# A two-layer graph kernel: the output's normalisation on ScalarE, and a new order of the work around it

## What is computed

```python
# layer 0
mi, mj = x @ Wi.T, x @ Wj.T                  # 512 x 512 each
out = deg[:, None] * (mi + b) + a @ mj       # deg = row sums of a
h = layernorm(x + out)
# layer 1: 8 heads of 64
q, k, v = h @ Wq.T + bq, h @ Wk.T + bk, h @ Wv.T + bv
scores = (q @ k.T) / 8, masked where adj == 0
out = softmax(scores) @ v
y = layernorm(h + out @ Wo.T + bo)           # the output
```

## Time and profile before

| | |
|---|---|
| median of 3 runs (lowest, highest) | 2925.93 us (2925.61, 2926.91) |
| the profiled execution: its own time | 2926.99 us |
| its span, first to last instruction | 2925.2 us |
| granted TensorE clock, mean over the span | 0.996 |
| busy: PE / PEld / DVE / ACT / POOL | 97% / 84% / 77% / 64% / 64% |
| one step in the middle (1496.46 to 1541.22) | 44.76 us |
| store of 512 KB (`out<-hb`), issue to landing, median | 2.8 us |

### The profile page before, as it was taken

One profiled execution on the slowest core, in us unless ns is written; L12 is line 12 of the kernel. 1 busy time (PEld: TensorE's weight loads), 2 busy tenths in 40 slices (PEclk: granted clock), 3 DMA queues, 4 the chain that ended last, 5 costly groups with the idle time before them and its releaser, 6 DMA issues.

```text
span 2925.2 us, 59805 instructions
## 1 busy us (share of the span) xinstructions
PE 2845.6 (97%) x18584; PEld 2457.2 (84%) x18584; DVE 2258.0 (77%) x5774; ACT 1871.2 (64%) x4874; POOL 1883.9 (64%) x1794
## 2 busy tenths in 40 slices
PE   6999999999999999999999999999999999999997
PEld 5888888888888888888888888888888888888886
DVE  7687777777877877778778777777787787777776
ACT  4666666666666666666666666666666666666665
POOL 5667666576676675665766766657667667666573
PEclk9999999999999999999999999999999999999999
DMA  4333333333333333333233333333333332333321
GB/s 137 109 102 102 115 100 108 108 98 111 107 100 112 103 100 110 105 108 105 96 115 102 104 110 103 105 108 103 112 101 100 115 100 100 115 100 108 107 92 60
DMA packets 282405, 306.72 MB, mean 105 GB/s; under 512 B 18817, under 2 KB 214913, under 8 KB 282369
## 3 DMA queue, kind: packets, MB, share of 16 engines
q1 hardware_dynamic: 282368, 306.26, 32.1%
HBM read 173.55 MB, written 132.64 MB: 105 GB/s over the span
## 4 chain that ended last, share of the span: by engine, by line
POOL 36%; issue 31%; PE 23%; DVE 7%; POOLq 1%; ACT 0%; DMA 0%; DVEq 0%; SPq 0%
PE proj L535 12%; POOL pT_lo L400 10%; POOL xb L395 5%; PE proj L498 4%; POOL probs L391 4%; POOL xs_lo L368 3%; PE attn L660 3%; POOL oT_lo L423 3%; DVE hb L1145 3%; POOL hb L409 3%; POOL mj_lo L379 2%; PE av L498 2%; POOL xs_raw L352 2%; POOL xs_raw L349 1%; DVE pT_lo L1078 1%
## 5 line engine op out<-in xcount | busy, mean ns | idle before, releaser
L400 POOL TENSOR_TENSOR pT_lo<-pT_raw,pT_hi 128x512 fp32r<-128x512 f32 x315 | 403.3, 1297 | 402.7 <-ACT pT_hi L856 402.7
L825 ACT ACTIVATE probs<-probs,row_min 128x256 f32<-128x256 f32 x1024 | 509.0, 499 | 225.5 <-DVE row_min L1043 222.9
L391 POOL TENSOR_TENSOR probs<-probs,row_inv 128x512 f32<-128x512 f32 x256 | 266.9, 1043 | 434.1 <-DVE row_inv L1054 434.1
L1043 DVE CUSTOM_DVE_ANT_0 probs<-attn,mask_add 128x256 f32<-128x256 f32 x1024 | 375.9, 418 | 41.8 <-PE attn L660 39.8
L862 ACT COPY o_part<-av 64x512 f32<-64x512 f32 x256 | 149.6, 584 | 395.1 <-PE av L498 389.1
L535 PE MATMUL proj<-wji_hi,xs_hi 128*128 128x512 f32 x896 | 363.4, 406 | 14.7 <-DVE wji_lo L1222 10.8
L535 PE MATMUL proj<-wji_hi,xs_lo 128*128 128x512 f32 x896 | 355.6, 397 | 0.0
L535 PE MATMUL proj<-wji_lo,xs_hi 128*128 128x512 f32 x896 | 355.6, 397 | 0.0
L1074 DVE STREAM_TRANSPOSE probs<-probs 128x1024 f32<-128x1024 f32 x189 | 234.7, 1242 | 114.5 <-PE av L498 114.5
L616 PE MATMUL proj<-mj_hi,wq_hi 128*128 128x256 f32 x1024 | 293.4, 286 | 11.3 <-DVE mj_lo L997 11.3
L1145 DVE TENSOR_SCALAR hb<-hb,mean_var_out,rstd_out 128x512 f32<-128x512 f32 x128 | 156.4, 1261 | 188.1 <-POOL rstd_out L418 188.0
(11 more groups left out here) (126 smaller groups left out, 8611.2 us busy)
## 6 DMA issues: line engine op xcount, KB each, us to landing
bounce<-probs SPq DMA_DIRECT2D x189, 512.0 KB, 2.6
pT_raw<-bounce SPq DMA_DIRECT2D x756, 128.0 KB, 3.0
xs_raw<-in_xT SPq DMA_DIRECT2D x64, 512.0 KB, 4.1
xb<-in_x SPq DMA_DIRECT2D x64, 512.0 KB, 3.4
out<-hb SPq DMA_DIRECT2D x64, 512.0 KB, 2.8
w_raw<-in_w0T SPq DMA_DIRECT2D x8, 256.0 KB, 5.6
stage<-in_wqT SPq DMA_DIRECT2D x1, 1024.0 KB, 10.6
stage<-in_wkT SPq DMA_DIRECT2D x1, 1024.0 KB, 12.5
```

Source lines behind the costliest of these rows:

```text
L391: pool.tensor_tensor(e, e, inv, ALU.mult).then_inc(norm_odd_done, 1)
L400: pool.tensor_tensor(pT_lo[:, g % 2, :, :, i, :, :], pT_raw[:, g % 2, :, :, i, :, :], pT_hi[:, :, :, i, :, :].bitcast(F32), ALU.subtract). ...
L825: last = nc.scalar.activation(e, e, ACT.Exp, bias=row_min[:, g % 2, s:s + 1], scale=-1.0, accum_out=row_sum[:, g % 2, s:s + 1])
L1043: last = V.tensor_tensor_reduce(out=out_, in0=in_, in1=mask_, scale=1.0, scalar=MIN_CEILING, op0=ALU.add, op1=ALU.min, accum_out=row_min[: ...
```

## The change

The second layernorm's last operation moves from DVE to ACT. DVE computes `shift = -mean * rstd` (`norm_shift`, 128 x 2 numbers), and ACT then makes `rstd * hb + shift` with one instruction for each of the two rows of 128 (`norm_out`). All four compute engines also get a new order. On PE both transposes of `h` stand before the scores of pair 3, `attend` of pair 1 stands between the two halves of `q`, and `attend` of pair 2 before `v`. On POOL `root` of the output stands ahead of `add_bias`, and `residual` ahead of `x_low(b + 2, 1)`. The first of the two sums of `y` moves ahead of a `pt_low` on DVE; `h` is normalised between the two, as before. The numbers computed are the same.

```diff
@@ GpSimd step @@
-                if y_: split_o(b - 1, 3)
                 normalise_odd(b, 1)
                 normalise_odd(b, 0)
                 mj_low(n, 0)
+                if y_: split_o(b - 1, 3)
                 mj_low(n, 1)
...
                 p_low(b, 2, 1)
+                if y_: root("out", b - 1)
                 if ahead: add_bias(b + 2, parity)
-                if y_: root("out", b - 1)
                 if ahead: x_low(b + 2, 0)
+                split_o(b, 0)
                 p_low(b, 3, 0)
+                residual(n, 1 - parity, stored=y_)
                 if ahead: x_low(b + 2, 1)
-                split_o(b, 0)
                 split_o(b, 1)
                 split_o(b, 2)
-                residual(n, 1 - parity, stored=y_)
@@ TensorE step @@
                 attend(b, 0, not y_)
                 transpose_h(n, 0, 1 - parity)
+                transpose_h(n, 1, 1 - parity)
                 scores(b, 1, only=3)
-                transpose_h(n, 1, 1 - parity)
                 q(n, 0)
+                attend(b, 1)
                 q(n, 1)
-                attend(b, 1)
                 k(n, 0)
                 k(n, 1)
+                attend(b, 2)
                 v(n, 0)
-                attend(b, 2)
                 v(n, 1)
                 attend(b, 3)
@@ ScalarE: new, and step @@
+            def norm_out(n, parity):
+                act.wait_ge(shift_done, n + 1)
+                for r in range(R):
+                    nc.scalar.activation(hb[:, parity, r, :], hb[:, parity, r, :], ACT.Identity, bias=shift[:, r:r + 1],
+                                         scale=rstd["out"][:, r:r + 1]).then_inc(normed["out"], 1)
...
+                normalise_even(b, 1)
+                exponentials(b, 0)
+                mj_high(n, 0)
                 if y_: o_high(b - 1, 3)
-                exponentials(b, 0)
-                normalise_even(b, 1)
-                mj_high(n, 0)
                 normalise_even(b, 0)
...
                 exponentials(b, 3)
-                normalise_even(b, 3)
-                o_high(b, 0, not y_)
                 q_high(n, 0)
                 o_low_part(b, 1)
+                normalise_even(b, 3)
                 p_high(b, 2)
+                if ahead: x_high(b + 2, 0)
                 q_high(n, 1)
+                o_high(b, 0, not y_)
                 k_high(n, 0)
-                if ahead: x_high(b + 2, 0)
-                if ahead: x_high(b + 2, 1)
                 o_high(b, 1)
+                if y_: norm_out(b - 1, 1 - parity)
                 k_high(n, 1)
                 o_low_part(b, 2)
                 p_high(b, 3)
+                if ahead: x_high(b + 2, 1)
                 o_high(b, 2)
@@ VectorE: new, and step @@
             def norm_mean(which, n):
+                if which == "out" and not (type(n) is int and n == 0):
+
+                    dve.wait_ge(normed["out"], R * n)
+                    dve.nop(nofuse=True)
...
+            def norm_shift(n):
+                dve.wait_ge(rstd_done["out"], n + 1)
+                V.scalar_tensor_tensor(out=shift[:, :], in0=mean_var["out"][:, :, 0], scalar=-1.0, in1=rstd["out"][:, :],
+                                       op0=ALU.mult, op1=ALU.mult).then_inc(shift_done, 1)
...
                 if y_: v_low(b, 0)
-                if y_: o_sum(b - 1, 3)
                 maxima_of_head(b, 1, 0, not y_)
                 maxima_of_head(b, 1, 1, not y_)
+                if y_: o_sum(b - 1, 3)
                 l0_sum(n, U1, other)
+                maxima_of_head(b, 0, 0, not y_)
                 if y_: v_low(b, 1)
-                maxima_of_head(b, 0, 0, not y_)
                 maxima_of_head(b, 0, 1, not y_)
                 l0_sum(n, Z1, other)
+                inverse_sums(b, 1)
                 l0_sum(n, U2, other)
-                inverse_sums(b, 1)
...
                 hT_low(n, 1)
-                if y_: norm_stats("out", b - 1, 0, read["y"], hb_row[other])
                 maxima_of_head(b, 3, 1)
                 o_sum(b, 0, not y_)
+                if y_: norm_stats("out", b - 1, 0, read["y"], hb_row[other])
                 inverse_sums(b, 3)
                 if y_: norm_stats("out", b - 1, 1, read["y"], hb_row[other])
+                if y_: norm_mean("out", b - 1)
                 flip(b, 3)
                 q_low(n, 0)
                 o_sum(b, 1)
-                if y_: norm_mean("out", b - 1)
                 q_low(n, 1)
+                if y_: norm_shift(b - 1)
                 k_low_half(n, 0)
-                if y_: norm_apply("out", b - 1, hb_row[other])
                 o_sum(b, 2)
+                k_low_half(n, 1)
                 p_low(b, 3, 1)
-                k_low_half(n, 1)
@@ VectorE last_step @@
-                norm_apply("out", b - 1, hb_row[0])
+                norm_shift(b - 1)
```

More of the change, by code:

```diff
@@ L168, in build @@
         rstd = {k: sb(f"rstd_{k}", [P, R]) for k in ("h", "out")}
+        shift = sb("shift", [P, R])
         adj_i = xb[:, 1, 0, :].bitcast(I32)
@@ L223, in build @@
         normed = {k: sem(f"normed_{k}") for k in ("h", "out")}
+        shift_done = sem("shift_done")
         def probs_row(g, i, r, tail):
@@ L887, in step @@
                 pt_high(b, 0, 0, not y_)
+                pt_high(b, 0, 1, not y_)
                 exponentials(b, 2)
-                pt_high(b, 0, 1, not y_)
                 normalise_even(b, 2)
@@ L985, in last_step @@
                 o_high(b, 3)
+                norm_out(b - 1, 0)
             steps(act, step, last_step)
@@ L1150, in step @@
                 if y_: v_low(b, 0)
-                if y_: o_sum(b - 1, 3)
                 maxima_of_head(b, 1, 0, not y_)
                 maxima_of_head(b, 1, 1, not y_)
+                if y_: o_sum(b - 1, 3)
                 l0_sum(n, U1, other)
+                maxima_of_head(b, 0, 0, not y_)
                 if y_: v_low(b, 1)
-                maxima_of_head(b, 0, 0, not y_)
                 maxima_of_head(b, 0, 1, not y_)
                 l0_sum(n, Z1, other)
+                inverse_sums(b, 1)
                 l0_sum(n, U2, other)
-                inverse_sums(b, 1)
                 l0_sum(n, M2, other)
+                l0_sum(n, U3, other)
                 inverse_sums(b, 0)
-                l0_sum(n, U3, other)
                 l0_sum(n, Z2, other)
@@ L1170, in step @@
                 pt_low(b, 0, 0)
-                agg_sum(n, 1, other)
                 norm_stats("h", n, 0, read["agg"], h_row[other])
                 inverse_sums(b, 2)
+                agg_sum(n, 1, other)
                 norm_stats("h", n, 1, read["agg"], h_row[other])
                 norm_mean("h", n)
+                if y_: y_sum(b - 1, 0, other)
                 pt_low(b, 0, 1)
-                if y_: y_sum(b - 1, 0, other)
                 norm_apply("h", n, h_row[other])
```

## The result

The changed kernel takes **2972.36 us** (median of 4 runs, 2971.19 to 2973.26), the kernel before took 2926.42 in the same session (4 runs, 2925.61 to 2926.98). The ratio is 1.0157, with a 95% interval from 1.0139 to 1.0175: 1.6% slower, 46 us. The forecast was 2964, in a range of 2928 to 3008.

The account below looks back on a forecast made before the run. PE, busy 97%, was taken as the bound, with a 0.67 us stall at pair 3's `attend`. Terms 0.03 + 0.45 + 0.10 + 0.05 = +0.63 us a step, over 61 steps 38 us, gave 2964 us, range 2928 to 3008.

Parts of the forecast that it names:

- the case of the held `shift`: Main forecast: DVE's `shift` waits for POOL's running instruction, giving +0.63 us a step and 2964 us; chance 0.60.
- Rival 1: DVE's `shift` is not held and runs at once: -0.35 us a step, 2905 us; chance 0.15.
- shift held by `add_bias`: On DVE, `shift` waits for POOL's whole `add_bias`, until 1533.14; price bounded by 0.06 (not held) and 2.45 us (held).
- norm_out: On ACT, each of the two instructions takes 0.82 us, or 0.72 from start to start, bounds 0.53 and 1.0.
- The whole 0.67: PE's stall of 0.67 us a step at pair 3's `attend`, forecast to return whole, with `attend` 0.03 later than before.
- tight waits: On the way to `y`, the inverse sums and pair 0's `normalise_even` become tight: +0.05 us a step, bounds 0 and 0.15.
- `Z1`: Next step's seventh PE matmul waits for POOL's `xs_lo`, behind two `residual` instructions: +0.45 us, +0.10 for the restart.
- Pair 1's `attend`: On PE, it waits for POOL's `p_low` and pays a restart: +0.22 us, bounds 0 and 0.35, covered by a later wait.
- Rival 2: DVE's pair 3 `pT_lo` is held for one more POOL `residual`, 1.26 us: +1.35 a step, 3007 us; chance 0.15.
- the forecast's 0.07: Margin by which DVE reaches pair 3's `pT_lo` (1537.69) before POOL would start `residual` (1537.76).
- The last sign: POOL's `probs` of pair 3 starts some 25.4 us after `Z1`; otherwise the forecast fails.

Follow-up runs that it names:

- e1: Changed kernel with `shift` made by two one-column DVE instructions, each with one tensor input, instead of one two-column instruction with two tensor inputs: 2910.59 us, ratio 0.9939.
- e2: Changed kernel with POOL's `add_bias` split into two instructions of 512 columns instead of one of 1024: 2917.79 us, ratio 0.9965.
- e7: Changed kernel with `root` of the output put back behind `add_bias` on POOL: 3108.58 us, ratio 1.0617.
- e3: Changed kernel with `x_low(b + 2, 1)` put back ahead of `residual` on POOL, `shift` still held: 2942.01 us, ratio 1.0048.
- e5: Changed kernel with e1's one-column `shift` and e3's `x_low` ahead of `residual` together: 2898.53 us, ratio 0.9899.
- e6: e5 with pair 1's `attend` back behind both halves of `q`, and `o_low_part(b, 1)` behind `normalise_even(b, 3)` on ACT: 2888.88 us, ratio 0.9863.
- e11: Changed kernel's order, but the output normalised on DVE by its pair of 512-column instructions, without `norm_out` or `shift`: 2978.68 us, ratio 1.0173.

## Why the prediction was right

**Direction and size.** +38 us was forecast, +46 measured. The forecast chose the case of the held `shift`, and e1 shows that this was the fork: without the hold the same kernel is faster than before. Rival 1 had been worked out as 2905; e1 measured 2911.

**shift held by `add_bias`.** Forecast until 1533.14, a row of 2.4; measured 2.34, ending 0.02 after `add_bias`. e2 and e7 vary it with POOL's instruction.

**norm_out.** Forecast 0.82 each, 0.72 from start to start; measured 0.81 and 0.71 (1.42 for the pair, 1465.54 to 1466.96).

**The whole 0.67 returns at pair 3's `attend`.** Right in kind, too small in size. Forecast was that `attend` starts 0.03 later than before, plus the 0.05 of tight waits. Apart from `Z1`'s delay it came 0.24 later. `shift` ends 0.05 later than its chain gave, which uses up the 0.05 of tight waits. The difference of 0.16 comes behind it. `k_hi` was costed at 0.74, and takes 0.84 to the start of `o_part`. DVE's `pT_lo` needs 0.61 behind POOL's, not 0.55. This mis-sized sum is the one real miss: 0.16 x 61 is 10 us. The 0.05 of the next point partly cancels it, which leaves 0.11 a step, 7 of the 8 us between forecast and result.

**`Z1`.** Forecast 0.45 + 0.10; measured 0.38 and 0.12, 0.50. POOL was held 0.50 by DVE's `pT_lo` instead of 0.41. e3 shows that this stall goes with `residual`'s place, and e1 that with `residual` still there, but no hold, only 0.14 is left: it takes both.

**Pair 1's `attend`.** Forecast +0.22, measured 0.19, and 0.18 by e5 against e6. The forecast said that it would not matter because a later wait takes it up. That holds in the changed kernel; it stops holding once that wait is gone, as in e5.

**Rival 2** (DVE late for its port) did not come in the changed kernel's trace: DVE's `pT_lo` is written at 1470.22 and POOL's `residual` at 1470.24, so the forecast's 0.07 had become 0.02. But the margin isn't what decides. In e7 it was down to 0.01 and nothing was lost; in two steps of e2 it was 0.25 and the race was lost, at 7.9 us a step. The rival's price, one `residual` more, was far too low, and that it stayed away was in part luck.

**The last sign.** POOL's `probs` of pair 3 was to start some 25.4 after `Z1`; it starts 25.52 after it (1430.15 to 1455.67), 0.10 of it `Z1`'s restart.

**What the forecast didn't see.** The store of the output as a condition for `residual` was named only as an argument against rival 2. In the changed kernel it has only 0.20 us to spare, and e11 shows it as the bound of this order. And the clock's fall behind a long wait (e7) lies beyond any case that was forecast.
